# State-space convolution ahead of attention: tile shapes of the convolution matmuls, stores of the kernels from ScalarE, first Toeplitz rows in three pieces, part of the start on GpSimd

## The chip, the cores and the metric

One NeuronCore of a Trainium2 chip. The time is that of one execution on the device in microseconds; of several runs the median is given. One execution was also taken with the hardware profiler. The engines are called PE (TensorE), DVE (VectorE), ACT (ScalarE), POOL (GpSimd) and SP (SyncE, which here only issues transfers).

## The reference, cut to what matters

`x` has shape (32, 64, 1024): batch, 64 channels, 1024 positions. Four steps follow one another: a long convolution along the positions, attention over the 64 channels, a channel mix by condition, and a feed-forward layer with experts. The change touches the first step alone:

```python
dt = exp(log_dt); A = -exp(log_A_real) + 1j * A_imag; dtA = A * dt
Cs = C * (exp(dtA) - 1) / A
K  = 2 * einsum('hn,hnl->hl', Cs, exp(dtA[:, :, None] * arange(1024))).real   # one kernel per channel
y  = causal_convolution(u * mask, K) + u * mask * D                           # by FFT in the reference
y  = y * mask
```

So for each of the 64 channels (heads h) there is a kernel of 1024 values, built from 64 complex modes, and every batch row is convolved with its channel's kernel.

## The kernel before, in words

The whole program is five instruction streams, one per engine, written out by hand and joined by semaphores. The stages run one behind the other: convolution, QKV projection with rotary embedding, attention, feed-forward. Each stage's function is called once per engine at the end of `build` (lines 1466 to 1505).

**Kernels of the channels.** A channel's 1024 values are a product of two tables: position = 32 a + b, and `ltab` holds the powers for the steps of 32 (with the coefficient multiplied in), `rtab` those for the single steps. Eight channels form a group g, so there are eight groups. `phases` (DVE, L399 to L406) makes the phases and rounds them, `exponents` (POOL, L360) and `magnitudes` (ACT, L337) the magnitudes, `sines` (ACT, L342) sine and cosine, `tables` (DVE, L444 to L450) the products, `kernels_pe` (PE, L459 or L462) the matmul, `kernels_out` (DVE, L474 to L481) the copy from PSUM with the skip term D added, and `store_kernels` (SP, L487) writes four pieces to the DRAM tensor `kpad`. Every row of `kpad` begins with 127 zeros, so that a load whose partition stride is one element gives a Toeplitz matrix.

**The coefficient** 2 C (exp(dtA) - 1) / A is needed once, for all channels. `decay_rates` (ACT, L328 to L332) gives exp and tanh, `phase_rates` (DVE, L381 to L392) reduces the angle, `first_magnitudes_and_sines` (ACT, L349 to L352) gives the sines and the squares, and `first_tables` (DVE, L415 to L436) does 22 operations of 128 x 64 elements behind the phases of group 0. `chain` marks an operation whose successor on DVE waits for it.

**Convolution.** Two channels of a group form a pair n; there are 32 pairs. One channel of the pair lies on partitions 0 to 63 and the other on 64 to 127, and each has its own PSUM bank. `load_toeplitz` (SP, L509, L512) brings two Toeplitz pieces of 64 rows and 1088 columns into a ring of three; `load_x_conv` (SP, L499) brings x for two pairs into a ring of two. In `conv_loads`, SP walks over the pairs: it waits for the stores of the pair's channel, at n % 4 = 3 it stores the next group's kernels, it loads the pair's Toeplitz pieces (which wait until pair n-3 has been used), then at even n x for a pair further on, and at n = 6, 10 and 14 weights of the next stage (512 KB each).

`convolve` does the pair's matmuls. d counts the distance in blocks of 128 positions, c the half block. `wide` (L541) uses a stationary tile of 64 x 128 for each channel, `narrow` (L552) two of 64 x 64, which fill the four quarters of the array; both stream (8 - d) x 32 columns, so from 256 columns at d = 0 to 32 at d = 7. The records of the profile show every f32 matmul as two. Even pairs take wide for d < 4 and then narrow; odd pairs take narrow first and then wide, with the first wide tile split into two halves of 128 columns:

```python
wide(pe, n, 0, 0, start=False, end=NJ // 2)
wide(pe, n, 0, 0, start=False, first=NJ // 2)
wide(pe, n, 1, 0, start=False)
```

Behind each pair, DVE multiplies by the mask (`conv_masks`, L625) into a ring of two, ACT writes the high part (`conv_hi`, L654, L655) and POOL the low part (`conv_lo`, L664, L665). PE may run three pairs ahead of the mask. The tables of group g + 2 are made beside the pairs of group g.

**Start.** `conv_matmuls` makes the kernels of group 0, then runs filler matmuls on the identity (`keep_busy`, L589): five of 256 columns, a wait for the first store, four more. Pair 0 waits for `ld_near` (columns 0 to 575 of its Toeplitz rows, L509) and, before its narrow tiles, for `ld_toep[0]` (the rest, L512).

Of the kernel before, what the change touches and what calls it, by code (L numbers as in the profile page):

```python
# [14 lines left out]
P = 128  # L15
# [82 lines left out]
def build(nc, x_conv, x_nat, lens, cond, modes, d_skip,  # L98
          w_qk, w_v, w_o, w_cond, w_ffn, w_b, consts, out):
    ctx = ExitStack()  # L100
    with ctx:
# [105 lines left out]
        def spare(name, part, j, shape):  # L207
# [53 lines left out]
        ld_near = signal("ld_near")  # L261
# [12 lines left out]
            "g_zero", "v_cidx", "v_len", "v_valid")]  # L274
        g_mag, a_mag, v_ph, v_round, a_sin, v_tab = [signal(n) for n in (
# [25 lines left out]
        def bank(n):  # L301
# [4 lines left out]
        names64 = ("dt", "ar", "rho", "rho32", "th", "k", "r", "vr", "v32", "e1", "tanh", "sh", "ch",  # L306
                   "cm1", "nr", "ni", "den", "t0", "t1", "t2", "gr", "gi", "cr", "ci")
# [18 lines left out]
        def decay_rates(act):  # L326
# [5 lines left out]
            act.activation(M("tanh"), M("rho"), ACT.Tanh, scale=0.5).then_inc(a_set, 1)  # L332

# [11 lines left out]
        def first_magnitudes_and_sines(act):  # L345
# [5 lines left out]
            act.activation(M("k"), M("ar"), ACT.Square).then_inc(a_set, 1)  # L351
            act.activation(M("t2"), AIM, ACT.Square).then_inc(a_set, 1)  # L352
            sines(act, 0)

        def exponents(gp, g):
            if 2 * g > 0:
                gp.wait_ge(v_tab, 2 * g)
            hs = slice(g * HGRP, (g + 1) * HGRP)
# [4 lines left out]
        def first_exponents(gp):  # L363
            gp.memset(zeros, 0.0).then_inc(g_zero, 1)
            gp.memset(d_at[:], 0.0).then_inc(g_zero, 1)
            gp.wait_ge(ld_cst, 16)
            gp.wait_ge(v_rho, 1)
            exponents(gp, 0)

# [39 lines left out]
        def first_tables(v):  # L409
# [3 lines left out]
            v.wait_ge(a_set, 8)  # L413

            v.scalar_tensor_tensor(M("cm1"), M("sh"), -2.0, M("sh"), ALU.mult, ALU.mult)  # L415
            v.scalar_tensor_tensor(M("tanh"), M("e1"), 1.0, M("tanh"), ALU.add, ALU.mult)
            v.scalar_tensor_tensor(M("t1"), M("sh"), 2.0, M("ch"), ALU.mult, ALU.mult)
            chain(v, v.tensor_tensor(M("k"), M("k"), M("t2"), ALU.add))
            v.scalar_tensor_tensor(M("t0"), M("cm1"), 1.0, M("tanh"), ALU.add, ALU.mult)
            v.tensor_tensor(M("ni"), M("t1"), M("e1"), ALU.mult)  # L420
            chain(v, v.reciprocal(M("den"), M("k")))
            chain(v, v.tensor_tensor(M("nr"), M("t0"), M("cm1"), ALU.add))
            v.tensor_tensor(M("t1"), M("ni"), AIM, ALU.mult)
            v.tensor_tensor(M("t0"), M("nr"), M("ar"), ALU.mult)
            v.tensor_tensor(M("t2"), M("ni"), M("ar"), ALU.mult)
# [1127 lines left out]
```

## Time and profile before

| | us |
|---|---|
| median of 3 runs (lowest, highest) | 908.87 (907.57, 912.06) |
| the profiled execution, its own time | 910.42 |
| span of its instructions | 906.8 |
| PE busy | 880.2 (97%) |
| DVE busy | 445.3 (49%) |
| POOL busy | 395.7 (44%) |
| ACT busy | 202.5 (22%) |
| convolution, first to last matmul | 25.11 to 171.35 |

The difference of 3.6 us between the execution's time and the span lies around the instructions. A row of the timeline gives the start, the busy time, engine and line, the operation, output <- inputs, shapes, how many instructions are merged, and in brackets the idle time before and what ended it. A row of the chain gives start, duration and what the end of the program depended on at that time. Idle time of an engine other than the last one awaited costs nothing by itself.

### The profile page before, as it was taken

The numbers are of one execution on the slowest core, as the hardware profiler recorded it, in microseconds if no ns is written. First come the engines' busy times: TensorE is split into PE (matmuls) and PEld (weight loads), VectorE is DVE, ScalarE is ACT, GpSimd is POOL, SyncE is SP. The second block draws the span as 40 slices with busy tenths as digits, with TensorE's granted clock in tenths as the row PEclk, the third lists the DMA queues.
The fourth block names the chain that finished last, engine by engine and source line by source line (L and its number), as shares of the span: only waits on it lengthen the run. The fifth ranks groups of instructions, "written<-read, shape, count | busy, mean of one in ns | idle before, by whom it ended". The sixth has DMA issues, their size and how long they took to land.

```text
span 906.8 us, 24930 instructions
## 1 busy us (share of the span) xinstructions
PE 880.2 (97%) x11054; PEld 766.1 (84%) x11054; DVE 445.3 (49%) x931; ACT 202.5 (22%) x365; POOL 395.7 (44%) x294
## 2 busy tenths in 40 slices
PE   2999999999999999999999999999999999999998
PEld 2898999988888888888777777777789999999998
DVE  6656572111222222258887777788533444334444
ACT  4445542100000000023122222233331101011110
POOL 1344564302555556569978878877511000000000
PEclk9999999999999999999999999999999999999999
DMA  2788778312224223156544454543452121212201
GB/s 66 184 220 211 184 187 187 83 59 69 70 70 106 70 72 79 48 175 181 142 136 135 152 159 153 159 153 120 133 175 89 56 93 52 90 71 71 84 35 70
DMA packets 83243, 105.35 MB, mean 116 GB/s; under 512 B 41664, under 2 KB 54592, under 8 KB 83136
## 3 DMA queue, kind: packets, MB, share of 16 engines
q1 hardware_dynamic: 82624, 103.24, 39.2%
q8 instruction: 87, 1.43, 0.7%
q0 software_dynamic: 512, 0.53, 0.2%
q14 instruction: 20, 0.16, 0.1%
HBM read 74.08 MB, written 29.65 MB: 114 GB/s over the span
## 4 chain that ended last, share of the span: by engine, by line
PE 93%; DMA 2%; DVE 2%; SPq 1%; issue 1%; POOL 1%; ACT 0%; DVEq 0%; POOLq 0%
PE ps L835 24%; PE ps L1297 21%; PE ps L1107 20%; PE ps L541 9%; PE ps L799 5%; PE ps L552 4%; PE ps L1063 3%; PE ps L1043 3%; PE ps L1270 2%; PE ps L1320 1%; DMA kpad<-ksb 1%; PE ps L1321 1%; DMA xc<-in_dram 1%; DMA toep<-kpad 0%; PE ps L462 0%
## 5 line engine op out<-in xcount | busy, mean ns | idle before, releaser
L1297 PE MATMUL ps<-wb,xf 128*128 128x420 f32 (+1 forms) x1152 | 195.7, 330 | 0.0
L1297 PEld LDWEIGHTS ps<-wb,xf 128*128 128x128 f32 x1152 | 188.2, 188 | 2.9 <-issue 0.2
L835 PE MATMUL ps<-y_hi,w_hi 128*128 128x512 f32 x320 | 125.1, 391 | 0.0
L835 PE MATMUL ps<-y_hi,w_lo 128*128 128x512 f32 x320 | 124.5, 389 | 0.0
L835 PE MATMUL ps<-y_lo,w_hi 128*128 128x512 f32 x320 | 124.5, 389 | 0.0
L1107 PE MATMUL ps<-y_hi 128*128 128x512 f32 x256 | 103.0, 402 | 0.2 <-POOL y_lo L970 0.2
L541 PE MATMUL ps<-xc,toep 64*128 64x192 f32 (+4 forms) x1088 | 97.8, 330 | 3.5 <-DMA xc<-in_dram 1.4
L1107 PE MATMUL ps<-y_hi,y_lo 128*128 128x512 f32 x256 | 100.2, 392 | 0.0
L1107 PE MATMUL ps<-y_lo,y_hi 128*128 128x512 f32 x256 | 100.2, 391 | 0.0
L541 PEld LDWEIGHTS ps<-xc,toep 64*128 64x128 f32 x1088 | 89.8, 187 | 6.8 <-issue 2.7
L942 POOL TENSOR_TENSOR rot<-rot,cst 128x512 f32<-128x512 f32 x40 | 52.7, 1318 | 73.1 <-DVE rot L913 73.1
L1148 POOL TENSOR_TENSOR sc<-sc,stat 128x1024 f32<-128x1024 f32 x32 | 65.6, 2050 | 33.3 <-DVE stat L1144 33.3
L835 PEld LDWEIGHTS ps<-y_hi,w_hi 128*128 128x128 f32 x320 | 60.1, 188 | 12.7
L835 PEld LDWEIGHTS ps<-y_lo,w_hi 128*128 128x128 f32 x320 | 60.1, 188 | 12.4
L835 PEld LDWEIGHTS ps<-y_hi,w_lo 128*128 128x128 f32 x320 | 60.1, 188 | 12.4
L913 DVE LOAD_MASK_SELECT rot<-ps x40 | 0.6, 14 | 141.7 <-PE ps L835 141.7
L1134 POOL TENSOR_TENSOR sc<-sc,stat 128x1024 f32<-128x1024 f32 x32 | 61.1, 1910 | 8.5 <-DVE stat L1130 7.9
L664 POOL TENSOR_TENSOR y_lo<-ym,y_hi 128x256 fp32r<-128x256 f32 x32 | 29.5, 920 | 75.8 <-ACT y_hi L655 75.7
L1125 DVE SCALAR_TENSOR_TENSOR sc<-ps,causal 128x1024 f32<-128x1024 f32 x32 | 39.1, 1223 | 40.1 <-PE ps L1043 40.1
L1107 PEld LDWEIGHTS ps<-y_hi 128*128 128x128 f32 x256 | 48.0, 188 | 12.3 <-issue 0.8
L1107 PEld LDWEIGHTS ps<-y_hi,y_lo 128*128 128x128 f32 x256 | 48.0, 188 | 10.5 <-issue 0.3
L625 DVE TENSOR_TENSOR ym<-ps,valid 128x512 f32<-128x512 f32 x32 | 22.1, 690 | 69.0 <-PE ps L552 52.5
(149 smaller groups left out, 1296.2 us busy)
## 6 DMA issues: line engine op xcount, KB each, us to landing
toep<-kpad SPq DMA_DIRECT2D x62, 272.0 KB, 4.6
xc<-in_dram SPq DMA_DIRECT2D x32, 256.0 KB, 5.2
q_rows<-rf SPq DMA_DIRECT2D x32, 256.0 KB, 2.6
q<-q_rows SPq DMA_DIRECT2D x16, 512.0 KB, 3.9
xr<-in_dram SPq DMA_DIRECT2D x16, 512.0 KB, 4.4
x_scratch<-xr SPq DMA_DIRECT2D x16, 512.0 KB, 2.6
x<-x_scratch SPq DMA_DIRECT2D x16, 512.0 KB, 3.6
out_dram<-x SPq DMA_DIRECT2D x15, 512.0 KB, 2.6
```

Of the source, the lines that this page charges most:

```text
L541: mm = pe.matmul(ps[:, 2 * (n % 3) + r, first * NB:end * NB], toep[rows, n % TR, at:at + P], xc[rows, n // XH % XR, 1 - c, n % XH, (first ...
L552: mm = pe.matmul(ps[half * HALF:(half + 1) * HALF, 2 * (n % 3) + r, d * NB:NJ * NB], toep[rows, n % TR, at:at + HALF], xc[rows, n // XH % ...
L664: gp.tensor_tensor(y_pair(1, n, 0), ym_pair(n, 0), y_pair(0, n, 0).bitcast(F32), ALU.subtract)
L799: mm = pe.matmul(out, wv[a][:, j, h * P:(h + 1) * P], y[b][:, j, b0:b1, s0:s1], start=(j == 0 and a + b == 0), stop=(j == NJ - 1 and a == 1))
L835: mm = pe.matmul(kq_bank(n), w[a][:, j, :], yt[b][:, j, g * 512:(g + 1) * 512], start=(j == 0 and a + b == 0), stop=(j == NJ - 1 and a == 1))
L942: gp.tensor_tensor(r, r, across(C("sin"), 8), ALU.mult).then_inc(g_rsin, 1)
L1043: mm = pe.matmul(ps[G * S:(G + 1) * S, g, rep * S:(rep + 1) * S], q_sb[i % 2][rows, b, G * REP + rep, :], kc[rows, i % 2, G, b * S:(b + 1) ...
L1107: mm = pe.matmul(ps[:, 6 + n, :], heads, wo(c, t)[:, n, :], start=(at == 0), stop=(at == 3 * NQT - 1))
L1125: v.scalar_tensor_tensor(sc[:, u % CR, :].rearrange("p (g k) -> p g k", g=4), ps[:, 0:4, 0:256], INV_SQRT, across(causal[:].rearrange("p r ...
L1134: gp.tensor_tensor(sc_groups(u), sc_groups(u), along(stat[:, u % CR, 0, :], S), ALU.subtract).then_inc(g_sub, 1)
L1148: gp.tensor_tensor(sc_groups(u), sc_groups(u), along(stat[:, u % CR, 2, :], S), ALU.mult).then_inc(g_prob, 1)
L1297: mm = pe.matmul(joint_bank(i, piece)[:, 0:hi - lo], xf[i % 2][:, a, t, :], wb[t][:, w4_place(t, c), lo:hi], start=(t == 0 and a + c == 0) ...
```

## The change

- The coefficient is rearranged. ACT makes the two squares of |A|^2 earlier and a third square (sh2); POOL does 14 operations of 128 x 64 (`first_factors`) behind its exponents of group 0, with five internal waits; DVE keeps a reciprocal and eight operations. The product `rtab` of group 0 goes from DVE to POOL. `tables` waits for each sine by itself instead of for all three.
- The kernels of the groups 1 to 7 are stored by ACT: group 1 behind the y copies of pair 0, the others ahead of the copies of pairs 4, 8, ..., 24. Group 0's stay on SP.
- The Toeplitz rows of pair 0 come in three pieces (columns 0 to 319, 320 to 575, 576 to 1087) for each channel, one channel from SP, the other from ACT, which issues its three between the magnitudes and the sines of group 1. `ld_mid` is new.
- In `conv_loads`, x is loaded ahead of the wait for the kernels' store and ahead of the Toeplitz pieces; the weights come at n = 7, 11 and 15.
- Of the 16 tiles (d, c) the first nine are wide and the last seven narrow, in place of eight and eight. Odd pairs begin with the first tile, (0, 0), as narrow, then their seven narrow ones, then eight wide ones; nothing is split.
- Fillers: two of 256 columns, 34 of 32 columns (on 32 columns of the array), the wait for the first store, one of 256.

```diff
         def first_exponents(gp):
...
             exponents(gp, 0)
+            first_factors(gp)
+            gp.wait_ge(a_mag, 2)
+            gp.wait_ge(a_sin, 3)
+            gp.tensor_tensor(rtab, rn[:, 2, :], mg[:, 1, :], ALU.mult).then_inc(g_rtab, 1)
+        def first_factors(gp):
+            gp.wait_ge(a_set, 6)
+            gp.tensor_tensor(M("den"), M("den"), M("aim2"), ALU.add).then_inc(g_den, 1)
+            gp.tensor_tensor(M("em"), M("e1"), M("tanh"), ALU.mult)
+            gp.tensor_tensor(M("u"), AIM, CRE, ALU.mult)
+            gp.tensor_tensor(M("ua"), M("ar"), CIM, ALU.mult)
+            link(gp, gp.tensor_tensor(M("w"), AIM, CIM, ALU.mult))
+            gp.tensor_tensor(M("em"), M("em"), M("tanh"), ALU.add)
+            link(gp, gp.tensor_tensor(M("u"), M("u"), M("ua"), ALU.add))
+            gp.tensor_tensor(M("tanh"), M("e1"), M("e1"), ALU.add)
+            link(gp, gp.tensor_tensor(M("ua"), M("ar"), CRE, ALU.mult))
+            link(gp, gp.tensor_tensor(M("w"), M("w"), M("ua"), ALU.subtract))
+            gp.wait_ge(a_set, 9)
+            gp.tensor_tensor(M("sh2"), M("sh2"), M("e1"), ALU.mult)
+            link(gp, gp.tensor_tensor(M("sh"), M("sh"), M("ch"), ALU.mult))
+            gp.tensor_tensor(M("em"), M("em"), M("sh2"), ALU.subtract)
+            gp.tensor_tensor(M("sh"), M("sh"), M("tanh"), ALU.mult).then_inc(g_fac, 1)
...
         def first_tables(v):
-            v.wait_ge(a_set, 8)
...
+            v.wait_ge(g_den, 1)
+            chain(v, v.reciprocal(M("den"), M("den")))
+            v.wait_ge(g_fac, 1)
+            v.scalar_tensor_tensor(M("u"), M("u"), 2.0, M("den"), ALU.mult, ALU.mult)
+            chain(v, v.scalar_tensor_tensor(M("w"), M("w"), 2.0, M("den"), ALU.mult, ALU.mult))
+            v.tensor_tensor(M("t0"), M("sh"), M("u"), ALU.mult)
+            v.tensor_tensor(M("t1"), M("em"), M("w"), ALU.mult)
+            v.tensor_tensor(M("th"), M("sh"), M("w"), ALU.mult)
+            chain(v, v.tensor_tensor(M("k"), M("em"), M("u"), ALU.mult))
             v.tensor_tensor(M("cr"), M("t0"), M("t1"), ALU.add)
+            chain(v, v.tensor_tensor(M("ci"), M("th"), M("k"), ALU.subtract))
...
+        FIRST_ROWS = [(0, 2 * P + HALF), (2 * P + HALF, NJ // 2 * P + HALF), (NJ // 2 * P + HALF, L + HALF)]
+        def load_first_toeplitz(eng, r):
+            eng.wait_ge(st_zero, 16)
+            eng.wait_ge(st_k[0], 16)
+            for (lo, hi), landed in zip(FIRST_ROWS, (ld_near, ld_mid, ld_toep[0])):
+                load_rows(eng, 0, r, lo, hi, landed)
...
         def conv_loads(sp):
...
             store_kernels(sp, 0)
-            sp.wait_ge(st_zero, 16)
-            for n in range(S // 2):
+            load_first_toeplitz(sp, 0)
+            for n in range(1, S // 2):
                 g = n // GP
-                sp.wait_ge(st_k[g % 2 * GP + n % GP], 16 * (g // 2 + 1))
-                if n % GP == 3 and g + 1 < NHG:
-                    store_kernels(sp, g + 1)
-                load_toeplitz(sp, n)
                 t = (n - TR + 1) // XH + XR - 1
                 if n - TR + 1 > 0 and (n - TR + 1) % XH == 0 and t < S // 2 // XH:
                     load_x_conv(sp, t)
+                sp.wait_ge(st_k[g % 2 * GP + n % GP], 16 * (g // 2 + 1))
+                load_toeplitz(sp, n)
...
+        TILES = [(d, c) for d in range(NJ) for c in range(2)]
+        WIDE, NARROW = TILES[:NJ + 1], TILES[NJ + 1:]
...
             else:
-                for d in range(NJ // 2, NJ):
-                    for c in range(2):
-                        mm = narrow(pe, n, c, d, start=(d == NJ // 2 and c == 0))
-                wide(pe, n, 0, 0, start=False, end=NJ // 2)
-                wide(pe, n, 0, 0, start=False, first=NJ // 2)
-                wide(pe, n, 1, 0, start=False)
-                for d in range(1, NJ // 2):
-                    for c in range(2):
-                        mm = wide(pe, n, c, d, start=False, stop=(d == NJ // 2 - 1 and c == 1))
+                for d, c in [WIDE[0]] + NARROW:
+                    mm = narrow(pe, n, c, d, start=((d, c) == WIDE[0]))
+                for d, c in WIDE[1:]:
+                    mm = wide(pe, n, c, d, start=False, stop=((d, c) == WIDE[-1]))
...
         def conv_matmuls(pe):
             kernels_pe(pe, 0)
             pe.wait_ge(ld_cst, 16)
-            keep_busy(pe, 5)
+            keep_busy(pe, 2, 2 * P)
+            keep_busy(pe, 34, HB)
             pe.wait_ge(st_k[0], 16)
-            keep_busy(pe, 4)
+            keep_busy(pe, 1, 2 * P)
...
         def conv_hi(act):
             magnitudes(act, 1)
+            load_first_toeplitz(act, 1)
             sines(act, 1)
...
+                if n % GP == 0 and 0 < g < NHG - 1:
+                    store_kernels(act, g + 1)
...
+                if n == 0:
+                    store_kernels(act, 1)
```

## Rows read from the trace of the kernel before

**Rows 1.** Windows: stretch, length, busy time (instructions) of PE, PEld, DVE, ACT, POOL, granted clock, DMA share, GB/s
```profile
17.06:25.11 8.05, 7.26 (x22) 5.83 (x23) 5.59 (x17) 3.42 (x6) 1.19 (x2) 1.00 0.25 60
25.11:171.35 146.24, 142.32 (x3193) 134.44 (x3193) 75.37 (x131) 63.96 (x106) 72.07 (x77) 1.00 0.79 192
```
**Rows 2.** The chain in order of time, start of the program
```profile
9.56 1.10 DVE rn L406 x3
...
11.59 0.47 DVE t L421
...
14.30 0.14 DVE t L434
...
14.61 0.23 DVE t L436
14.87 0.44 DVE rn L444
...
16.67 0.35 DVE ph L450
...
19.05 2.13 DMA kpad<-ksb
...
21.78 3.19 DMA toep<-kpad
```
**Rows 3.** Timeline of all engines, start of the program
```profile
0.88 0.10 POOL L365 MEMSET d_at<- 128x16 f32 x1
...
4.86 1.19 POOL L360 TENSOR_TENSOR mg<-t,cst 128x256 f32<-128x256 f32 x2 [3.87 <-DVE t L382]
4.87 0.65 DVE L384 TENSOR_SCALAR t<-t 128x64 f32<-128x64 f32 x1
```
**Rows 4.** Timeline of PE, fillers ahead of the first pair
```profile
18.93 0.63 PE L589 MATMUL ps<-cst 128*128 128x256 f32 x1
19.35 0.63 PE L589 MATMUL ps<-cst 128*128 128x256 f32 x1
...
22.34 0.47 PE L589 MATMUL ps<-cst 128*128 128x256 f32 x1
```
**Rows 5.** Timeline of PE, the first wide records of an odd pair
```profile
105.83 0.38 PE L541 MATMUL ps<-xc,toep 64*128 64x128 f32 x2
106.05 0.39 PE L541 MATMUL ps<-xc,toep 64*128 64x128 f32 x4
106.27 0.50 PE L541 MATMUL ps<-xc,toep 64*128 64x128 f32 x4
106.60 0.38 PE L541 MATMUL ps<-xc,toep 64*128 64x256 f32 x2
106.82 0.54 PE L541 MATMUL ps<-xc,toep 64*128 64x224 f32 x3
```
**Rows 6.** The chain, narrow records of two pairs, wide records of two pairs
```profile
103.31 2.60 PE ps L552 x128
105.91 5.84 PE ps L541 x68
```
**Rows 7.** The chain around pair 12, and PE's longest wait of the convolution
```profile
65.49 6.89 DMA kpad<-ksb
...
74.48 6.70 DMA xc<-in_dram
...
PE ps L541 <- DMA xc<-in_dram: 1.4, 1, 1.4
```
**Rows 8.** DMA issues up to 175 us: KB each, median us to landing
```profile
prm<-in_dram SPq DMA_DIRECT2D x2, 80.0 KB, 2.4
```
**Rows 9.** Timeline of ACT, pairs 4 and 5
```profile
48.74 0.65 ACT L654 ACTIVATE y_hi<-ym 128x256 fp32r<-128x256 f32 x1 [3.55 <-DVE ym L625]
...
51.90 1.28 ACT L342 ACT_TABLE_LOAD   x1
53.20 1.31 ACT L342 ACTIVATE rn<-rn,cst 128x256 f32<-128x256 f32 x3
```

More of the change, by code:

```diff
@@ L274, in build @@
             "g_zero", "v_cidx", "v_len", "v_valid")]
+        g_set, g_den, g_fac, g_rtab = [signal(n) for n in ("g_set", "g_den", "g_fac", "g_rtab")]
         g_mag, a_mag, v_ph, v_round, a_sin, v_tab = [signal(n) for n in (
@@ L332, in decay_rates @@
             act.activation(M("tanh"), M("rho"), ACT.Tanh, scale=0.5).then_inc(a_set, 1)
+            act.activation(M("den"), M("ar"), ACT.Square).then_inc(a_set, 1)
+            act.activation(M("aim2"), AIM, ACT.Square).then_inc(a_set, 1)
         def magnitudes(act, g):
@@ L411, in first_tables @@
             phases(v, 0)
-            v.wait_ge(a_set, 8)
[L415 to L425, printed above, removed]
-            chain(v, v.tensor_tensor(M("k"), M("nr"), AIM, ALU.mult))
-            v.tensor_tensor(M("gr"), M("t1"), M("t0"), ALU.subtract)
-            chain(v, v.tensor_tensor(M("gi"), M("t2"), M("k"), ALU.add))
@@ L505, in load_toeplitz @@
                 sp.wait_ge(pe_conv, n - TR + 1)
-            near = NEAR if n == 0 else 0
-            if near:
-                for r in range(2):
-                    sp.dma_start(toep[r * HALF:(r + 1) * HALF, n % TR, 0:near],
-                                 bass.AP(kpad, head(n, r) * (KROW + 1), [[1, HALF], [1, near]])).then_inc(ld_near, 16)
             for r in range(2):
-                sp.dma_start(toep[r * HALF:(r + 1) * HALF, n % TR, near:],
-                             bass.AP(kpad, head(n, r) * (KROW + 1) + near, [[1, HALF], [1, L + HALF - near]])).then_inc(ld_toep[n % TR], 16)
+                load_rows(sp, n, r, 0, L + HALF, ld_toep[n % TR])
         def conv_loads(sp):
@@ L528, in conv_loads, with wide @@
                     load_x_conv(sp, t)
+                sp.wait_ge(st_k[g % 2 * GP + n % GP], 16 * (g // 2 + 1))
+                load_toeplitz(sp, n)
                 for part in range(2):
-                    if n == W_FIRST + 4 * part:
+                    if n == W_FIRST + 1 + 4 * part:
                         sp.dma_start(wraw[:, part, :], w_v[:, part * NJ * P:(part + 1) * NJ * P]).then_inc(ld_w[0], 16)
-                if n == W_FIRST + 8:
+                if n == W_FIRST + 9:
                     sp.dma_start(wraw[:, 2, :], w_qk[0]).then_inc(ld_w[2], 16)
-        def wide(pe, n, c, d, start, stop=False, first=None, end=NJ):
+        def wide(pe, n, c, d, start, stop=False):
             at = d * P + (1 - c) * HALF
-            first = d if first is None else first
             for r in range(2):
                 rows = slice(r * HALF, (r + 1) * HALF)
-                mm = pe.matmul(ps[:, 2 * (n % 3) + r, first * NB:end * NB], toep[rows, n % TR, at:at + P],
-                               xc[rows, n // XH % XR, 1 - c, n % XH, (first - d) * NB:(end - d) * NB],
+                mm = pe.matmul(ps[:, 2 * (n % 3) + r, d * NB:NJ * NB], toep[rows, n % TR, at:at + P],
+                               xc[rows, n // XH % XR, 1 - c, n % XH, 0:(NJ - d) * NB],
                                start=start, stop=stop)
```

69 lines of the change are left out of this document (38 added, 31 removed).

## The prediction

> **What bounds the kernel now.** I read the stretches first: from the first convolution matmul at 25.11 to the last the matrix engine is busy for 142.32 us of 146.24 [rows 1]. Nothing in the diff touches what follows, and the page's chain is 93% PE over the whole span, so a microsecond gained before 171.35 moves everything behind it. The edits can act in three places: the start, where PE waits, the matmuls of the convolution, and its few waits. The chain of the start comes next [rows 2]: DVE work up to 17.06, then PE's first kernels, the store to kpad (19.05 to 21.18), the Toeplitz load (21.78 to 24.97), first convolution matmul 25.11. Then the convolution: 36 records of an odd pair and 32 of the following even pair take 5.84 us [rows 6], so PE runs record behind record, and the waits list holds one wait worth naming, 1.4 us for xc [rows 7].
>
> The terms are made against the profiled execution (910.42 us, span 906.8), which is 1.55 us above the median of 908.87; the difference found is then taken off the median.
>
> **Start, vector chain.** Before, DVE ends its phases at 10.66 (9.56+1.10) and PE starts at 17.06: 6.40 us. 22 small operations and the five table products lie between. After, DVE does a reciprocal (0.47 to 0.55, with its link 0.59), two products by the reciprocal (0.14 unlinked, 0.26 linked: 0.40), four (3 x 0.14 + 0.26 = 0.68), two (0.40): 2.07 us. Of the table products, four stay on DVE: 14.87 to 16.66 is 1.79 us, with the handover of 0.05 1.84; the fifth, rtab (0.40, from 16.66 to 17.06), goes to POOL. Sum 3.91, against 6.40: 2.5 us less if nothing else moves [rows 2]. Two more short ACT squares stand ahead of the magnitudes, in ACT's wait for POOL's first product: nothing. The third, sh2, follows the half-angle sine and is needed by POOL's eleventh operation only; I take it as ready by then.
>
> What POOL does in exchange is 14 operations of 128x64, from 6.05 on, and the trace has none of that kind. Bounds: 0.10 us (its MEMSET of 16 columns) and 0.61 (its product of 256 columns) [rows 3]. I take 0.23, that is 0.10 and a quarter of the other 0.51, since both rows grow with columns: 14 x 0.23 = 3.2 us, five links of about 0.1, so factors are ready near 10.2 if undisturbed and DVE need not wait. But it does not go undisturbed: DVE's 128x64 operation that starts with POOL's product at 4.87 takes 0.65, one that runs alone 0.23 [rows 2, 3]. DVE has seven linked small operations and eight of 256 columns in 6.1 to 10.66. I charge half of a POOL operation for each of the seven (0.7) and a whole one (0.16 of pitch) for the last four POOL operations (0.6): 1.3 us; and 0.4 for the rtab product of about 0.6 us that falls onto DVE's last small operations. Net gain 2.5 - 1.3 - 0.4 = 0.8 us. Ends: 2.5 gained, and 1.5 lost with POOL operations of 0.61 (factors at 6.05 + 14 x 0.61 = 14.6, plus 0.4+0.7+0.4+1.8 = 17.9, and some blocking on top).
>
> The Trainium skill, in "SBUF — State Buffer", section "SBUF: two separate sides", says that a GpSimd operation and a DVE operation with two SBUF inputs or in a two-port mode take one shared port pair for the whole instruction and the loser blocks fully. By that rule the sum for this part would be the same 0.8 or less; it speaks against moving small products to POOL, and the row of 0.65 us agrees.
>
> **Start, first Toeplitz rows.** From PE's start to the first convolution matmul it is 8.05 us. The store to kpad stays on SP, and lands 4.1 us after PE's start. Then, before, two loads of 144 KB go out one behind the other, the second at 21.78, 0.60 after that landing (0.52 of it the first's issue), and it lands 3.19 later. After, SP and ACT issue one 80 KB load each at the same time: 0.52 gained, and the load is smaller; 80 KB lands in 2.4 us, 144 KB in 3.2 [rows 2, 8]. With two at once I take 2.8: 0.4 gained. ACT is free: its magnitudes of group 1 follow POOL's two products (1.19 us [rows 3]) from PE's start, so they are done before the store lands. Sum 0.9 (ends: 0 if ACT's issue is slow, 1.3). The other pieces go out some 0.6 and 1.2 us later on each queue and are needed after 8 and 16 passes, 1.6 and 2.8 us into the convolution (a pass of 256 columns is 0.216 [rows 5], shorter ones in proportion): hidden. On ACT three issues, 1.8 us if ACT needs 0.6 like SP, now stand ahead of a table load and three sines of group 1 (1.28 and 1.31 [rows 9]), so the sines end 4.4 us after the store landed; DVE's products (1.8) follow, and PE wants them when pair 0 ends, 2.9 + 4.2 us after that landing: 0.9 us to spare, nothing, and if they were late, PE's kernels of group 1 would wait.
>
> PE's fillers must not be longer than this wait. At the start a 256-column record takes 0.42 us (18.93 to 19.35), the 1.2 GHz level; the first short record is at 22.34, 5.3 us after PE started, and behind it PE is at 2.4 GHz, with granted clock 1.00 throughout [rows 1, 4]. After: kernels and two fillers of 256 end 2.7 us after PE's start, then come 68 records of 32 columns. At columns alone they take 0.053 each at the lower level: 3.6 us, so all end at 6.4, and one more filler (0.43) at 6.8; the rows land at 7.1. Just hidden: nothing.
>
> **Convolution matmuls.** Columns and tiles are the same; a tile of 128 columns (d=4, c=0) turns wide in each pair. A wide pass of 128 columns takes 0.11 (106.05 to 106.27 is two), its columns alone 0.107, so the move costs at most 0.01. The odd pairs lose the split of the first wide tile: four passes of 128 columns (0.44 without the change of form) for two of 256 (0.43). What I count is the change from 64x64 to 64x128 tiles, once per odd pair. Now a 128-column pass follows it, and the next starts 0.22 later (105.83 to 106.05) where the ones after take 0.11: 0.10 us in which the next weights were not there. After, a 256-column pass comes first, which lasts 0.216 anyway (106.60 to 106.82) and covers that load: 16 x 0.10 = 1.6 us [rows 5]. Ends 0 (the loss only moves to the record behind) and 2.4 (0.15 each).
>
> The Trainium skill, in "TensorEngine Tiling (Array Packing)", section "Tiling Modes" under its key properties, says that changing the tiling mode drains TensorE. As many changes remain, so by the page alone this term would be 0 and the whole gain 3.1; the trace agrees that a change costs, and shows in which pass.
>
> **Waits of the convolution.** Before, at 65.49 the stores of a group are issued on SP's queue behind 512 KB of weights and two 256 KB loads, and land 6.89 us later, at 72.38; SP sits on that wait, so Toeplitz goes out after it and x last, its second half at 74.48, landing 6.70 later at 81.18: PE waits 1.44 us [rows 7]. After, x is issued ahead of the wait, the stores go out on ACT, and the weights at an odd n, where no x is loaded. x would go out before 72.4, so over 1.4 us earlier: the wait is gone. 1.4 us gained. ACT's four issues (0.6 each as above, 2.4 us) fall in its wait of 3.55 us for the next mask: nothing while under 3.5 us; above, the y copies come late [rows 9]. Behind the x loads Toeplitz goes out 1.3 us later, needed two pairs later (8.4 us), landing in about 5: covered except under the weights. Ends: 0.5 lost, 2.3 gained.
>
> Six more semaphores cost nothing I can see a row for. **Sum**: 0.8 + 0.9 + 1.6 + 1.4 = 4.7 us: 905.7 for the profiled execution, 904.2 against the median. Half a per cent, about what a measurement here can tell, is 4.5 us: the boundary is at 904.3.
>
> **Rivals.**
> - POOL gives it all back: small operations nearer 0.61 than 0.10, DVE blocked behind them. 4.7 - 0.8 - 1.5 = 2.4 gained: 906.5. For it speaks the 0.65 us row; against it the 0.10 one.
> - Fillers of 32 columns don't bring PE to its upper level before the first pairs. 5.3 us at half speed lose 2.65: 906.8. Before, PE rose under 256-column records only.
> - The change doesn't do what it says in the convolution: the bytes are the same with the transfers near their bound, the xc wait reappears elsewhere and the form change costs as before. 1.7 gained: 907.2.
> - More goes than named: with stores off SP the queue never runs dry, and half of the other slow places of this stretch (142.32 busy; 16 x 8.44, that is 2.60 for 128 narrow records and 5.84 for 68 wide ones, is 135.0 [rows 6]) go: 3 more, 901.2.
> - Slower: the 68 filler records. They decide once they last longer than 4.0 us, 0.06 each. If each costs what a record costs behind a change of form (0.22), with PE staying at the lower level, they take 15.0 us, 11 beyond the cover: 904.2 + 11 = 915.2. Weights of 32 columns behind one another are in no row.
>
> **Numbers.** Forecast 904.2, chance 0.44 (its own range 902.7 to 905.7); POOL 0.13; lower level 0.08; unchanged convolution 0.12; more 0.16; slower 0.07. Range 900.6 to 909.0: from the fourth rival to the ends where start and waits gain nothing, leaving the fillers and mishaps out. Faster by over 0.5%: the fourth and somewhat over half of the forecast, 0.41; slower 0.07; the rest 0.52.
>
> **What would show it.** PE's first record at about 16.3, the first convolution matmul 7.1 us later; POOL 128x64 near 0.2 us; DVE's small operations before 10 longer than 0.23; first wide pass of an odd pair followed after 0.216; no PE wait on xc; x issued before Toeplitz; kpad landing within 3 us. A first pair of twice 2.8 us for its wide part, POOL operations above 0.4, fillers ending after the rows land, or a new wait of PE on ld_toep or on tables would prove me wrong.

## The result and the profile after

The changed kernel takes 905.66 us (median; 905.37 to 905.99), the kernel before, timed beside it, 908.87 (906.88 to 912.06). The ratio is 0.9948 with an interval of 0.9927 to 0.9969, so 0.5% or 3.2 us faster, on the boundary between "within 0.5%" and "faster". The forecast was 904.2, 4.7 us less.

| | before | after |
|---|---|---|
| profiled execution, its own time, us | 910.42 | 905.51 |
| span, us | 906.8 | 903.7 |
| PE's first matmul | 17.06 | 15.89 |
| from there to the first convolution matmul | 8.05 | 6.71 |
| first convolution matmul to first matmul of the next stage | 146.17 | 144.73 |
| from there to the last matmul | 731.87 | 732.38 |

The two executions differ by 4.9 us, their spans by 3.1, the medians by 3.2. The execution of before spent 3.6 us around its instructions, the one of after 1.8, so the spans are the better pair. The start gave 2.5 us (1.17 + 1.34), the convolution 1.4; the stages behind it lost 0.5 and the time behind the last matmul 0.3. Of the 1.17, 0.07 is that the inputs landed sooner in this execution (DVE's first operation at 4.18, before at 4.25).

The same two windows as [rows 1], for the kernel after:

```profile
15.89:22.60 6.71, 6.49 (x79) 5.24 (x79) 3.75 (x12) 2.22 (x4) 1.19 (x2) 1.00 0.23 57
22.60:167.33 144.73, 141.35 (x3065) 132.94 (x3065) 77.42 (x135) 65.15 (x109) 72.06 (x77) 1.00 0.77 194
```

**The start.** The chain of the kernel after, in order of time, answers to [rows 2]:

```profile
11.52 0.47 DVE t L448
...
13.12 0.61 issue
...
13.98 0.43 DVE rn L465
...
15.89 1.24 PE ps L486 x4
...
17.88 0.34 SPq L514
...
19.75 2.72 DMA toep<-kpad
...
22.60 1.48 PE ps L569 x11
```

DVE ends its phases at 11.52, not at 10.66 as before, and still PE starts 1.17 us earlier. Then the loads: the near Toeplitz pieces go out 3.86 us after PE's start (before 21.78 - 17.06 = 4.72) and land in 2.72 (before 3.19). That is the 1.34. What sets the 3.86 is not the store's landing any more: group 0's first store was issued at 17.88, ACT's Toeplitz load goes out at 19.35, and the last one, SP's at 19.75, stands behind SP's own four store issues of 0.34 to 0.43 us. What holds DVE back shows in the timeline of POOL and DVE (first two lines POOL alone, then POOL's last product, then DVE), which answers to [rows 3]:

```profile
5.94 0.32 POOL L388 TENSOR_TENSOR t<-t 128x64 f32<-128x64 f32 x1
6.21 0.32 POOL L389 TENSOR_TENSOR t<-t 128x64 f32<-128x64 f32 x1
...
13.00 0.72 POOL L376 TENSOR_TENSOR ph<-rn,mg 128x256 f32<-128x256 f32 x1 [2.10 <-ACT rn L345]
```
```profile
10.23 1.29 DVE L440 SCALAR_TENSOR_TENSOR rn<-rn,ph 128x256 f32<-128x256 f32 x3
...
13.08 0.72 DVE L456 TENSOR_TENSOR t<-t 128x64 f32<-128x64 f32 x1
```

POOL's small operations start 0.27 us apart. DVE's line L440 takes 1.29 us beside them (1.10 before), and its 128x64 addition at 13.08 takes 0.72 beside POOL's rtab product, where others like it take 0.22.

**The convolution.** The waits of PE in it, the largest (us in total, times, longest), answer to the wait of [rows 7]:

```profile
PE ps L489 <- DVE ph L475: 1.7, 3, 1.0
PE ps L569 <- issue: 0.7, 1, 0.7
PE ps L569 <- DMA toep<-kpad: 0.7, 1, 0.7
```

The wait for xc is gone. Two new ones stand there: for the tables (ph L475), 1.0 us ahead of pair 3, and for Toeplitz rows at pair 8. The chain of the kernel after around pairs 2 to 4 and at pair 8:

```profile
35.11 1.19 PE ps L580 x56
...
36.94 0.97 DVE rn L465
37.91 0.03 issue
37.94 1.12 DVE rn L465
39.06 0.02 issue
39.08 1.02 DVE rn L466
...
41.06 0.42 DVE ph L475
41.48 0.04 issue
41.52 0.72 PE ps L489 x8
...
52.69 7.74 DMA toep<-kpad
```

Each product of L465 takes 1.0 to 1.1 us where the same line takes 0.43 at 13.98 and the last one, L475, takes 0.42. POOL is the neighbour: its y_lo products of pairs 1 and 2 run from 36.65 to 40.85 without a break. They meet the tables because the y copies of pair 1 on ACT are late, behind this (timeline of ACT):

```profile
28.86 2.04 ACTq L514 DMA_DIRECT2D kpad<-ksb  x4
30.93 1.28 ACT L340 ACT_TABLE_LOAD   x1 [1.96 <-issue]
...
35.47 0.64 ACT L684 ACTIVATE y_hi<-ym 128x256 fp32r<-128x256 f32 x1
```

The stores of group 1 hold ACT for 2.04 us and push the table loads, sines and pair 1's copies back. Counted over the whole convolution, the slots in which PE makes the kernels of groups 1 to 7 (undisturbed 0.45 each) took about 5.0 us in all before and 7.3 after; the 32 pairs without these slots took 141.2 before and 137.5 after. (Sums like these depend by 0.1 or 0.2 us on where a slot is taken to begin.) So the pairs gained 3.8 us and these slots gave 2.3 back: 1.28 at pair 3, 0.3 at pair 15 and 0.6 at pair 19, while those at pairs 7, 11 and 23 changed by 0.25 or less each way.

### The profile page after: what moved, and what is told of

The parts are those of the page before. It is cut to its first block, busy times and chain, and to the rows that moved or that the text cites. A ratio compares the mean times of both kernels' runs of the same rounds, so it can differ in the third digit from the quotient of the medians.

```text
span 903.7 us, 24817 instructions
## 1 busy us (share of the span) xinstructions
PE 878.7 (97%) x10982; PEld 763.9 (85%) x10982; DVE 445.1 (49%) x917; ACT 202.7 (22%) x366; POOL 401.0 (44%) x309
## 4 chain that ended last, share of the span: by engine, by line
PE 92%; DVE 3%; DMA 1%; issue 1%; POOL 1%; SPq 0%; ACT 0%; DVEq 0%; POOLq 0%
PE ps L867 24%; PE ps L1329 21%; PE ps L1139 20%; PE ps L569 9%; PE ps L831 5%; PE ps L580 4%; PE ps L1095 3%; PE ps L1075 3%; PE ps L1302 2%; DMA toep<-kpad 1%; PE ps L1352 1%; PE ps L1353 1%; DVE rn L465 1%; PE ps L489 0%; DVE rn L466 0%
## 5 line engine op out<-in xcount | busy, mean ns | idle before, releaser
L1139 PEld LDWEIGHTS ps<-y_lo,y_hi 128*128 128x128 f32 x256 | 48.1, 188 | 9.7 <-issue 0.4
```

The lines of the kernel that those rows point to most:

```text
L1139: mm = pe.matmul(ps[:, 6 + n, :], heads, wo(c, t)[:, n, :], start=(at == 0), stop=(at == 3 * NQT - 1))
```

## The experiments

Each result stands against the kernel before, timed in the same series. The kernel before had medians of 910.71 (E1 to E4), 909.29 (E5 to E8) and 909.83 (E9 to E12).

| | median (range) us | ratio (interval) |
|---|---|---|
| E1 before + tiles | 910.17 (908.87 to 913.83) | 0.9999 (0.998 to 1.0019) |
| E2 after, vector chain of before | 906.73 (906.02 to 908.56) | 0.9959 (0.9944 to 0.9974) |
| E3 after, stores on SP | 906.80 (904.85 to 907.82) | 0.9950 (0.9932 to 0.9968) |
| E4 after, SP's order of before | 905.00 (903.84 to 905.54) | 0.9936 (0.9914 to 0.9959) |
| E5 after, no small fillers | 904.84 (904.49 to 907.61) | 0.9955 (0.9939 to 0.9972) |
| E6 after, group 1 stored by SP | 904.96 (904.51 to 906.44) | 0.9962 (0.9947 to 0.9977) |
| E7 E6 + tables a pair earlier | 903.91 (902.67 to 904.59) | 0.9942 (0.9925 to 0.9959) |
| E8 before + stores on ACT | 910.20 (907.63 to 913.22) | 1.0016 (1.0003 to 1.0028) |
| E9 before + new start | 907.95 (904.1 to 913.6) | 0.9989 (0.9969 to 1.0010) |
| E10 after, once more | 905.56 (904.7 to 907.58) | 0.9955 (0.9940 to 0.9970) |
| E11 E7, SP's order of before | 903.97 (902.91 to 907.59) | 0.9942 (0.9920 to 0.9963) |
| E12 before + weights at odd n | 910.20 (906.94 to 913.03) | 1.0004 (0.9986 to 1.0023) |

### E1: the tile shapes alone

```diff
-                wide(pe, n, 0, 0, start=False, end=NJ // 2)
-                wide(pe, n, 0, 0, start=False, first=NJ // 2)
...
+                for d, c in [WIDE[0]] + NARROW:
+                    mm = narrow(...)
+                for d, c in WIDE[1:]:
+                    mm = wide(...)
```

> The kernel before with the new tile shapes alone (nine wide, seven narrow tiles; odd pairs begin with tile (0, 0) as narrow; nothing split). My theory of the prediction: a 256-column pass behind the change of form covers the next weights, 16 x 0.10 = 1.6 us less, 907.3. The rival, that the loss belongs to the change of form itself and goes on behind whatever pass is first (the trace of the changed kernel has the second pass 0.32 us after the first instead of 0.216): odd pairs 4.25 instead of 4.26 us, even pairs 4.18, and 0.2 us or nothing in the time, 908.7.

No change: 0.9999. The interval (0.998 to 1.0019) is too wide to exclude 1.6 us by itself; the records decide. An undisturbed odd pair takes 4.25 us where it took 4.26. The first wide records of an odd pair in the kernel after (timeline of PE; two matmuls of the tile at once, the second two 0.32 later):

```profile
37.64 0.49 PE L569 MATMUL ps<-xc,toep 64*128 64x256 f32 x2
...
37.96 0.57 PE L569 MATMUL ps<-xc,toep 64*128 64x256 f32 x4
```

0.32 us for 256 columns, where the pass behind takes 0.216 (37.957 to 38.173). The 0.10 us that stood behind the first 128-column pass in [rows 5] now stands behind the first 256-column pass. E1 has the same steps (31.501, 31.821, 32.037). It is no load of weights that a longer pass would cover; it comes with the change of form. The Trainium skill, in "TensorEngine Tiling (Array Packing)", section "Tiling Modes", says that a change of mode drains TensorE. The rows agree that each change costs, here 0.10 us. The term of 1.6 us falls.

One thing more is in this trace. E1 leaves SP's queue and the stores as before, and PE has no wait for xc in it: x for pair 12 lands at 81.30, as late as before (81.18), but PE, held up by stalls of 1.5 and 1.1 us and a wait of 0.8 for the mask, starts that pair only at 82.8. A wait that is missing from one trace is thus no proof that the transfer came sooner.

### E2: the vector chain of before in the kernel after

The functions of the start (`decay_rates`, `first_magnitudes_and_sines`, `first_exponents`, `first_tables`, `tables`, `kernels_pe`) are before's; POOL has no `first_factors`.

> The changed kernel with the start's vector chain as before: 22 small operations and all five table products on DVE, nothing of it on POOL. If the chain is worth what the two traces say, PE's first matmul comes at 17.1 instead of 15.9 and the time is 1.2 us more, 906.9. Rival: the earlier start is eaten up behind it by the waits for tables, and the time stays within 0.3 us of 905.7.

PE starts at 17.09 and not at 15.89: 1.2 us. The convolution starts at 24.49 and not at 22.60: 1.9 us. The other 0.7 lie behind PE's first kernels. The store to kpad landed 2.14 us after its issue, and the Toeplitz load took 3.06. With the new chain the store is quicker in every trace that gives its landing (E3 to E7 and E9 to E11: 1.39 or 1.40 us; in the kernel after it had landed by 19.35, within 1.47), with the old chain slow in every one (before, E1, E2, E8, E12: 2.13 to 2.26). So from PE's first matmul to the convolution the three pieces from two queues gave 8.05 - 7.40 = 0.65 us, and the quicker store, which comes with the vector chain, the other 0.7. Beside the slow stores, and beside none of the quick ones, the trace has a packet of another instruction queue (two lines of the DMA view of before, 19.0 to 21.2; with the new chain that packet comes at 27.3 to 28.6):

```profile
q1 hardware_dynamic: 240, 0.02, 7.8%
q14 instruction: 1, 0.01, 1.0%
```

That the packet delays the store's landing is likely from this and not tried. By the times E2 settles less: its median lies 4.0 us below that of before in its series, those of the changed kernel 3.2 and 4.3 in theirs, so no loss from the old chain can be told there.

### E3 and E4: who stores the kernels, and SP's order

E3 lets SP store at n % 4 = 3, the rest stays as after. E4 keeps the stores on ACT and gives SP its old order:

```diff
 E3
+                if n % GP == 3 and g + 1 < NHG:
+                    store_kernels(sp, g + 1)
 E4
-                t = (n - TR + 1) // XH + XR - 1
-                ... load_x_conv(sp, t)
                 sp.wait_ge(st_k[g % 2 * GP + n % GP], 16 * (g // 2 + 1))
                 load_toeplitz(sp, n)
+                t = (n - TR + 1) // XH + XR - 1
+                ... load_x_conv(sp, t)
-                    if n == W_FIRST + 1 + 4 * part:
+                    if n == W_FIRST + 4 * part:
```

> The changed kernel with the kernels of groups 1 to 7 stored by SP again, at n % 4 = 3 ahead of the Toeplitz rows; x still ahead, weights at odd n. Theory: the stores on ACT cost at group 1 (ACT issues 2.0 us of stores ahead of the tables' sines, PE waits 1.0 us for the tables of group 2) and were not needed to be rid of the wait for x; so PE's wait at about 40.5 goes, no long wait for xc comes back, and the time is 0.5 to 1.5 us less than 905.7. Rival: the stores' own queue is what removed the wait; then SP stands at st_k again, PE waits over 1 us for xc or toep near pairs 8 or 12, and the time is 906.5 to 908.5.

> The changed kernel with SP's order of before (x behind the Toeplitz rows, weights at n = 6, 10, 14), stores still on ACT. Theory: the order and the odd n of the weights took the wait of pair 12 away; with the old order PE waits again for xc near a pair with weights, 1 us or more, against the 0.66 us for toep at pair 8 that the changed kernel has: 905.9 to 907.5. Rival: the own queue of the stores did it all: no wait over 0.7 us, 905.2 to 905.8.

E3's waits in the convolution:

```profile
PE ps L571 <- issue: 0.9, 2, 0.4
PE ps L489 <- issue: 0.7, 1, 0.7
PE ps L582 <- DMA toep<-kpad: 0.6, 1, 0.6
PE ps L489 <- DVE ph L475: 0.4, 1, 0.4
```

With ACT free, the tables made beside pair 2 are on time: the slot at pair 3 is 0.45 us. Three of DVE's five products there take 0.42 and the last two 1.1, as in the kernel before; in the kernel after, four take 1.0 to 1.1. That confirms what made the wait of 1.0 us. No xc wait comes back, since x is ahead of the wait in SP's order, but Toeplitz rows (0.55 at 36.5) and issue stalls do, and the convolution is 145.73 us long, 1.0 longer than in the kernel after. E4 is 143.69 long. It has neither an xc wait nor the Toeplitz wait of pair 8, and 905.00 is no worse than the kernel after, and lower than E3 of the same series (all but one of E3's executions are above all of E4's). With the stores off SP's queue its old order does as well: the new order was not needed. Whether it brought the Toeplitz wait is not settled: E10, the changed kernel again, has none at pair 8 and one of 0.30 us at 96.0, and E11, with the old order, has two, of 1.35 and 0.3.

How far x is ahead of PE shows in the landing of its second half for pair 12 and the start of that pair: before 81.2 for 79.8 (where PE would have begun), E3 75.7 for 78.8, E4 76.2 for 77.9, the kernel after 74.9 for 78.4. Either edit, the stores off SP's queue or x ahead of the wait, is enough to be rid of the wait in the kernel with the new start. (Behind the convolution this execution of E4 spent 1.2 us more than that of the kernel after, so its span is no shorter: 903.7.)

### E5: no small fillers

```diff
-            keep_busy(pe, 34, HB)
```

> The changed kernel without its 34 fillers of 32 columns; the three of 256 columns stay. Theory: the 32-column fillers keep PE busy enough for the 2.4 GHz level to come before pair 0 (68 records at 0.053 us, then 0.032 us from 4.5 us after PE's start). Without them PE idles some 3 us ahead of pair 0 and begins it at 1.2 GHz: the wide records of pair 0 are twice as far apart for up to 5 us, the convolution ends 2 to 3 us later, 908 to 909. Rival: the fillers don't matter for the level, pair 0 runs at 2.4 GHz, the time stays within 0.5 us.

In its profiled execution (907.61) PE sat idle 2.12 us ahead of pair 0, and the wide records of pair 0, in the chain, took

```profile
22.39 5.35 PE ps L569 x36
```

against 3.31 us in the kernel after: until 26.4 the records were 0.39 us apart where they are 0.19 apart at 2.4 GHz, so the lower level cost 2.0. (The granted clock of the profile reads 1.00 in both stretches; the level is read from the distance of the records.) In the kernel after the 68 filler records are 0.053 us apart until 20.37 and 0.032 from there: PE reached the upper level 4.5 us after its start, under records of 32 columns. But the other executions of E5 took 904.49 to 905.03, as if nothing were lost. The fillers' worth is thus 2 us in one execution and nothing in three; what decides between them is open.

### E6 and E7: repairing the tables' wait

```diff
 E6 (conv_hi, conv_loads)
-                if n == 0:
-                    store_kernels(act, 1)
+                if n == 3:
+                    store_kernels(sp, 1)
 E7 (E6, and in conv_masks)
-                if k == 2 and g + 2 < NHG:
+                if k == 1 and g + 2 < NHG:
                     tables(v, g + 2)
```

> The changed kernel with the stores of group 1 alone on SP, behind the Toeplitz rows of pair 3; groups 2 to 7 on ACT. Theory: on ACT these stores (2.0 us of issue) push the sines of group 2 and the y copies of pair 1 back, POOL's low parts of pairs 1 and 2 then run without a break beside the five table products on DVE, which take 1.0 instead of 0.42 us each, and PE waits 1.01 us for them at 40.5. So that wait goes and the time is 0.7 to 1.2 us less than the changed kernel's. Rival: the wait comes from PE being earlier, not from ACT; it stays, and the time with it.

> As e6, and the tables of group g + 2 are made behind the mask of pair n % 4 = 1 instead of n % 4 = 2. Theory: the waits of PE for tables (kernels of groups 2 to 7 take 7.3 us in the changed kernel where 0.45 to 0.65 each is 3.5) are the new bound of this stretch; tables made a pair earlier take them away: 2.5 to 3.5 us less than the changed kernel, 902.5 to 903. Rival: DVE waits for ACT's sines there, the masks come late and PE waits for them instead; the time is within 0.5 us of e6 or above.

In E6 the slot at pair 3 falls from 1.73 to 0.73 us, but a wait of 0.95 for the Toeplitz rows of pair 1 comes at 27.7 and the convolution is 145.11 long. That wait can't come from the edit: the first instruction that differs is issued at 28.8. The same load landed at 27.3 in the kernel after and at 28.5 here. Without it the convolution would be 0.6 us shorter than after; the median (904.96) says neither one nor the other. In E7 the slots of groups 1 to 7 take about 5.2 us and not 7.3. E7's waits:

```profile
PE ps L571 <- DMA toep<-kpad: 1.1, 2, 0.9
PE ps L489 <- issue: 0.7, 3, 0.3
PE ps L571 <- issue: 0.6, 1, 0.6
```

The tables no longer appear with their own name; the largest wait is for Toeplitz rows, 0.9 us at 76.1. The convolution is 143.32 us, the median 903.91.

### E8: stores on ACT, alone

```diff
-                if n % GP == 3 and g + 1 < NHG:
-                    store_kernels(sp, g + 1)
+                if n % GP == 0 and 0 < g < NHG - 1:
+                    store_kernels(act, g + 1)
...
+                if n == 0:
+                    store_kernels(act, 1)
```

> The kernel before with the stores of groups 1 to 7 on ACT alone; SP's order, the start and the tiles as before. Theory, from e3 and e4 (906.8 with the stores on SP, 905.0 with SP's old order and the stores on ACT): the stores off SP's queue are the part of the change that shortens the convolution: no wait of 1.4 us for xc, fewer stalls of PE without a releaser, against 1 to 2 us of new waits for tables: 1.5 to 3 us less than the kernel before of the same call. Rival: without x ahead of the wait it gives nothing, within 0.7 us.

The xc wait is gone, and the kernel is no faster: 0.16% slower, with an interval that hardly leaves 1 out. But the wait is gone for the reason met in E1: x for pair 12 lands at 81.5, no sooner than before, and PE starts the pair only at 82.2. So E8 doesn't show that the stores' own queue brings x sooner; E4, with the new start, does (76.2). What made PE late is the more instructive part. The chain of E8 and, under it, that of before, at the same instruction of PE (the third piece of E8 is cut by the window's end):

```profile
49.99 1.26 PE ps L539 x13
51.25 2.07 issue
53.32 2.78 PE ps L539 x27
```
```profile
49.18 1.26 PE ps L541 x13
50.45 0.27 issue
50.71 5.03 PE ps L541 x52
```

PE stops behind the same 13 records, with no semaphore awaited, for 2.07 us in the one and 0.27 in the other (1.47 in E1). Such stalls fall at PE instructions a multiple of 256 apart, give or take missing records: counted in matmuls and weight loads, before's come at 1207, 2733, 3243 and 4006, which leave 183, 173, 171 and 166 over blocks of 256. The page of the kernel after has the queue that belongs to it:

```profile
q8 instruction: 87, 1.43, 0.7%
```

87 packets of 16 KB: the program's 21964 PE and PEld instructions in blocks of 256 would be 86. The trace gives each packet's time. In E8 one was under way from 50.6 to 51.8 and PE went on at 53.32; in before from 48.0 to 49.3, and PE went on at 50.71; in E1 51.8 to 52.9 and 54.38. In the convolutions of the fourteen traces PE has 31 stalls of over 0.15 us that the profile names issue. All have 151 to 185 instructions over, also in E5 and E9, where other fillers or tiles shift the count, and in 30 of them PE resumes 1.3 to 1.7 us behind the end of a packet, though packets come only every 6 us or so (2.1 us in the other). So PE had run out of instructions, and the length of the stall is how late the packet was. In E8 that packet began 10.0 us behind the one before it, in the kernel before 6.2.

One must not read too much into the count, though. The slots for the kernels of groups 2 to 7 stand 768 instructions apart, three blocks, so in the kernel after all of them have 156 over, and its waits at 113.2 and 131.1 (instructions 3996 and 4764), which the profile puts down to the tables, look like instruction stalls by the count. E5, whose slots have 20 over, has the same waits (1.7 us in three, the longest 1.0, as in the kernel after), so they are the tables'. In E7, whose tables are ready a pair earlier, stalls of 0.2 to 0.3 us for instructions stand at these places. The Trainium skill, in "Runtime: NRT & Kernel Launch", "Instruction fetch mechanics", says that instructions come in blocks of 16 KiB, 256 instructions, and that crossing a boundary is mostly hidden. The size agrees; at most of the 25 packets of a convolution nothing is seen, but at some it is not hidden, with 2.07 us at one boundary. The DMA queues of E8 in the microsecond ahead of the late packet (49.50 to 50.55; packets, MB, share of the 16 engines):

```profile
q1 hardware_dynamic: 98, 0.36, 89.3%
q10 hardware_dynamic: 186, 0.02, 14.1%
```

The engines are full with the loads of q1 and the stores of q10. That alone doesn't explain the delay: beside the packet of before, which came in time but for 0.27 us, q1 has 99.7% (47.9 to 49.4). What makes one packet late and another not was not found.

### E9, E10, E12: the start alone, the change again, the weights alone

E9 is before with the new start (vector chain, three pieces from two queues, fillers); the stores are SP's, order and tiles old. E10 is the changed kernel itself. E12 is before with

```diff
-                    if n == W_FIRST + 4 * part:
+                    if n == W_FIRST + 1 + 4 * part:
...
-                if n == W_FIRST + 8:
+                if n == W_FIRST + 9:
```

> The kernel before with the new start alone: POOL's factors and rtab, the three pieces of the first rows from SP and ACT, the 32-column fillers; stores, order, weights and tiles as before. Theory: since the tiles alone (e1) and the stores alone (e8) gave nothing, the start is the part that moves the time: PE's first matmul at 15.9, the convolution from 22.6 instead of 25.1, 2.5 us less than the kernel before of the same call. Rival: the earlier start is eaten up by waits in the convolution (transfers, tables, stalls without a releaser), and the time is within 0.8 us of before; then the parts work only together.

> The changed kernel itself, unedited, on the chip of this call, as the measure for e11 and for the others: 905.7 if the chips don't differ, PE's waits for tables again near pairs 3, 19 and 23, the wait for toep at pair 8, and at most two stalls without a releaser, whose places are whole multiples of 256 PE instructions apart.

> The kernel before with the three weight loads one pair later (n = 7, 11, 15) and nothing else. The stalls of PE without a releaser in the kernel before fall whole multiples of 256 PE instructions apart (16 KB, the size of one packet of the instruction queue), and the first two come while a weight load is under way. Theory: they are late instructions behind the loads; with the weights moved away from the pairs where x is loaded, the xc wait of 1.44 us and some of the stalls go, 1 to 2.5 us less than the kernel before of the same call. Rival: they only fall on other pairs, within 0.7 us.

E9 starts PE at 15.75 and the convolution at 22.59, as the kernel after does, and has the xc wait still (1.3 us at 78.1). Its profiled execution, 905.22 us, shows the 2.5 us of the start; its executions lie between 904.1 and 913.6, with a median 1.9 below before's, and the interval of the ratio includes 1. E10 repeats the result: 0.9955. In that same series it lies 2.4 us below E9 (905.56 and 907.95; all twelve executions of E10 are below E9's median), so the convolution's edits together are worth something that none of E1, E8 and E12 shows on the kernel before. E12 moves nothing. Its xc wait is gone too, with x for pair 12 at 78.6 for a start at 79.3, and in its place the profile has stalls for instructions of 1.17 and 1.15 us at 97.4 and 115.0. Before and each part alone (E1, E8, E9, E12) range over 4 to 10 us; the kernel after and E2 to E7 and E10 over 0.6 to 3.1, E11 over 4.7. So a part of the gain is that executions of 909 us and more no longer occur, and no single part does that.

### E11: E7 with SP's old order

The edit of E4 on top of E7's.

> e7 (tables a pair earlier, stores of group 1 on SP, the others on ACT) with SP's order of before and the weights at n = 6, 10, 14. e7 still waited for toep at pairs 8 and 12 (0.25 and 0.90 us), which e4 with the old order did not. Theory: both gains add, 902.7 to 903.3, over 2 us below the changed kernel of the same call. Rival: the old order brings the xc wait of pair 12 or stalls behind the weights back, and it is no better than e7, 903.7 to 904.5.

903.97, no better than E7. The tables are on time for longer (0.45 to 0.65 us in each of the seven slots, about 4 in all), but Toeplitz rows are late by 1.35 us at 54.3, and PE waits 0.18 for x at 41. Beside E10 on the same chip its median is 1.6 us lower, with ranges that overlap (902.91 to 907.59 and 904.70 to 907.58). E7 and E11 are faster than before by 0.6%, with 1 far outside their intervals; their ratio is also lower than the changed kernel's two (0.9948 and 0.9955), but by less than the intervals, so that they beat it is likely and not shown.

## Why the prediction was right in the total, and where it was wrong

The forecast was 4.7 us less, measured are 3.2 by the medians and 3.1 by the spans, inside the range of 900.6 to 909.0 and at the upper edge of the likeliest case (902.7 to 905.7). That the total is near is in part luck: one term came to nearly nothing, one was undone by what its edits cost elsewhere, and gains that no term named made up for them.

- **Vector chain, 0.8 forecast, 1.17 measured: right.** POOL's operations go out every 0.27 us where 0.23 was taken, DVE's phases end 0.9 us late where 1.3 was charged, rtab cost 0.5 (the 0.72 row) where 0.4 was. The half operation charged for each small DVE operation was too much: 0.7 charged, 0.36 measured. (Its "near 10.2" for POOL's factors is 9.8 by its own terms; they were ready at 10.9, and DVE needed them at 12.0.) The rival "POOL gives it all back" falls; E2's profile confirms the size.
- **First Toeplitz rows, 0.9 forecast, 1.34 measured: near by luck.** The loads went out 0.86 us earlier after PE's start and landed 0.47 faster. 2.8 us was taken for two at once, they took 2.72. But half of the 1.34 is no work of this edit. The term held that the store "lands 4.1 us after PE's start"; it landed within 3.5, 1.4 to 1.5 us after its issue rather than 2.1, as it does wherever the new vector chain is. In E2, with the old chain, the same edit gave 0.65: two loads at once took 3.06 and not 2.8. ACT's issues fitted in ahead of the sines of group 1, as predicted. The fillers ended just ahead of the rows (0.22 us idle), also as predicted, so the slower case and the case of the lower level did not occur.
- **Convolution matmuls, 1.6 forecast, 0.2 measured: wrong.** The failed step is "0.10 us in which the next weights were not there. After, a 256-column pass comes first ... and covers that load". The 0.10 us is paid whatever the length of the pass (37.64 to 37.96), and E1 is the same as before. The lower end, "the loss only moves to the record behind", is what happened.
- **Waits, 1.4 forecast: the mechanism right, its neighbours wrong.** The xc wait of 1.44 us went because x for pair 12 lands at 74.9 and not at 81.2, 3.5 us ahead of PE; its loads went out at 70.1 at the latest, ahead of 72.4 as the sum had it. E9, which keeps stores and order, keeps the wait (1.3 us). But the sentence that ACT's issues cost "nothing" failed at group 1: four store issues of 2.04 us in all push ACT's sines and copies, POOL's y_lo of two pairs falls together and DVE's products beside it go from 0.42 to 1.0 us. That costs 1.3 us in the slot at pair 3, and E3 takes it away by taking the stores off ACT; the later slots lost 1.0 more, and E5 shows that this is the tables too. And the Toeplitz rows behind x and weights, "covered except under the weights", were late by 0.66 at pair 8. E4, with SP's old order, has no such wait, but neither has E10 with the new one, so the cause is open.
- **What was not in the sum.** The pairs gained 3.8 us where terms three and four say 3.0. Of that 0.2 is the tiles and 1.4 the xc wait, less 0.66 for Toeplitz rows; the other 2.9 are a remainder: stalls named issue (0.27, 0.44, 0.62 and 0.33 before, 0.72 after) make 0.9 of it, the rest lies in records further apart than usual, for the most part in the same pairs (with their stalls, five pairs took 4.5 to 5.2 us before where 4.26 is undisturbed). This is the fourth rival (3 more), cancelled by the third (the loss reappears elsewhere): both happened. The prediction named the first as "slow places" without knowing what they were. That E8's stalls are longer, not shorter (3.2 us in two, before 1.65 in four), says that the reason it gave, that SP's queue never runs dry, is not enough.

Still open is which part makes the executions agree to 1 us, and why a packet of instructions is late in one execution and not in another.

## What to carry to other kernels

Where a stage is bound by PE with the DMA engines near full, a wait taken away comes back at the next late thing; so count, for each queue that a store is moved to, what its issues push back (here 2.04 us on ACT turned into 1.0 us of PE by way of POOL and DVE). Before a wait that is gone is booked as a gain, look whether the transfer landed sooner or the engine came later (E1 and E8). Read stalls named "issue" by PE's instruction count before judging an edit by them, and check that the place isn't at that count for another reason, as the kernel slots here are. And look whether a wait that is new begins ahead of the first changed instruction, as in E6. The start is the safer place: what was removed there (1.17 and 1.34 us) came through in each profile that has the new start whole.

## What the runs showed of the hardware

- PE stalls for instructions: up to 2.07 us (E8) at a block of 256, in 30 of 31 cases resumed 1.3 to 1.7 us behind the end of a 16 KB packet.
- An 8 KB store to DRAM lands 2.13 to 2.26 us after its issue in the five traces that have an 8 KB instruction packet beside it, 1.39 or 1.40 in the eight that have none and give its landing.
- The change from 64x64 to 64x128 tiles costs 0.10 us on the first pass, of 128 or of 256 columns (before, after and E1).
- A POOL product of 128x64 takes 0.32 us and the next starts 0.27 later; a DVE product of 256 columns goes from 0.42 to 1.0 or 1.1 beside a POOL product of the same size.
- PE rose to its upper level under filler matmuls of 32 columns too: 0.053 us apart, then 0.032 from 20.37 on. Without them one execution (E5) ran at the lower level for 4 us of pair 0, three showed no loss.
